# Last layer: the wide projections of the next sequence among the pairs of scores and values, half of the decays ahead of the query with its maxima

## The chip, the cores and the metric

The kernel runs on one core of a Trainium2 chip. The metric is the device time of one execution in microseconds (us). The engines are PE (TensorE, matrix products), DVE (VectorE), ACT (ScalarE), POOL (GpSimd) and SP (SyncE, here only a queue of transfers). Each executes its own instructions in order; semaphores tie them together.

## The reference

A residual stream `x` of 16 sequences, 256 rows each, 128 wide, goes through four layers. Only the last one is touched by the change. For each of its sequences the reference computes, cut to what matters:

```python
xn = layernorm(x)                                   # of the rows of this sequence
# a state space branch ("attn"): gives s
u, z = split(xn @ in_proj_w.T)                      # 256 channels each
xs   = silu(causal_conv4(u) + conv_b)
time_step, B, C = split(xs @ x_proj_w.T)            # 64, 16, 16
delta = softplus(softplus(time_step @ dt_proj_w.T + dt_b) + dt_b)
state_t = exp(delta_t * A) * state_(t-1) + (delta_t * xs_t) * B_t      # 16 states per channel
y  = (sum over states of state_t * C_t + xs * D) * silu(z);  s = y @ out_proj_w.T
# an attention block with experts ("ffn"): gives g
q, k, v = xn @ Wq + bq, ...;  rotary q and k;  16 heads of 8 columns
att = softmax(q k^T / sqrt(8)) v;   x1 = layernorm(xn + att @ Wo + bo) * g1 + be1
moe = top-2 of 8 experts: gelu(x1 @ W1 + b1) @ W2 + b2, weighted by the gates
g  = silu(layernorm(x1 + moe) * g2 + be2)
x  = x + s * g
```

The convolution over four steps is folded into four projections (`u_projT`), so that `u` is a sum of four products of 128 x 256 for each half of the channels, and `z` is one product for each half. The decays are `exp(delta * A)`: 16 states and 2 halves of the channels, which is 32 activations of 128 x 255 per sequence.

## The kernel before, in words

The last layer is `layer3`. A loop goes over the 16 sequences (four per turn of the hardware loop). One turn for sequence n finishes n and prepares n+1. The order of the work is written out by hand, one program per engine. PSUM is one tensor `bank` of eight banks; `back` is banks 0 to 3 and `front` banks 4 to 7. The stages, in order of time:

- **The front stage** (`attention_front` on PE, L2332). Query and key are turned (`turn_heads`, L2284), the scores of 4 blocks of 4 heads are computed (`scores`, L2302), and DVE takes the row maxima of each block (`heads_max`, L2780, 4 instructions). Then DVE finishes `delta` (`softplus_sum`, L2739, in `third_part`), and PE turns the query again, now with its maxima, which ACT copies (`copy_qm`, L2471).
- **The pair stage.** The heads are worked in 8 pairs, p = 0 to 7. PE computes transposed scores of a pair (`scoresT`, L2316, rows of 9), ACT takes the exponential (`exp_scores`, L2518) and behind it one group of four decays for one half of the channels (`decays`, L2510). PE makes the values of a block of two pairs (`heads_out`, L2374). Two sets of two banks alternate for the pairs, so `scoresT` of pair p waits for the exponential of pair p-2. Pairs 0 and 1 belong to the end of the turn before. Also in this stage: PE's `out_rows` (L2325), which gives `s`; ACT's copy of it (L2585), for which DVE waits before it updates `x` (L2923); then DVE's norm of the next sequence, whose last part writes `xn` (L2687), which PE turns after pair 5 (`turn_x`, L2247) and ACT copies after pair 6 (`copy_xnT`, L2468). Meanwhile DVE scans states 0 to 7 (`scan`, L2811) and multiplies by C (`times_c`, L2821).
- **The middle stage.** ACT copies the last values (L2561), PE turns them (L2412), DVE divides (L2845 to L2849), PE projects (L2419, L2423), then come the projections of `u` and `z` for sequence n+1 (`project_uz`, L2257 and L2261), then the first layer norm on DVE, the turning of `x1` (L2430), the router (L2434), and DVE's `route_shift` (L174).
- **The expert stage.** Eight experts, `up` (L2386), `gelu` (L2548) and `down` (L2397), beside the scans of states 8 to 15 and the preparation of n+1 up to `dt`.

PE's two calls around the change are these:

```python
for k in range(2, HP):
    scoresT(n, k)
    if k % 2 == 0:
        heads_out(k // 2 - 1)
    if k == 5:
        turn_x(n + 1, 1 - par)
```

Transfers: SP stores B and C of n+1 to DRAM and loads them broadcast; POOL adds groups of states by accumulating DMAs.

Of the kernel before, what the change touches and what calls it, by code (L numbers as in the profile page):

```python
# [15 lines left out]
P = 128  # L16
NSEQ, T, D = 16, 256, 128
TILES = T // P
# [2063 lines left out]
def layer3(nc, c):  # L2082
    w = c.w3
    with ExitStack() as ctx:
# [156 lines left out]
        def _(pe):  # L2241
# [11 lines left out]

            def project_uz():
                for i in range(CI):
                    for k in range(DCONV):
                        done = nc.tensor.matmul(bank[:, 2, i * T:(i + 1) * T], u_projT[:, i, k, :], xpad[:, k:k + T],  # L2257
                                                start=(k == 0), stop=(k == DCONV - 1))
                done.then_inc(u_in_psum, 1)
                for i in range(CI):  # L2260
                    done = nc.tensor.matmul(bank[:, 3, i * T:(i + 1) * T], z_projT[:, i, :], xnT,  # L2261
                                            start=True, stop=True)
                done.then_inc(z_in_psum, 1)
# [8 lines left out]
            def project_dt(m):  # L2272
                pe.wait_ge(xdbl_ready, m + 1)
                pe.wait_ge(zg_ready, m + 1)
                for i in range(CI):
                    done = nc.tensor.matmul(bank[:, 3, i * T:(i + 1) * T], dt_projT[:, i, :], xdbl[0:RANK, :],
                                            start=True, stop=True)
                done.then_inc(dt_in_psum, 1)
# [77 lines left out]
            for a in range(TILES):  # L2356
                qkv_rows(a)
            project_uz()
            project_x(0, 0)
            project_dt(0)  # L2360
            attention_front(0)
            with pe.Fori(0, NSEQ // 4) as m:
                for q in range(4):
# [50 lines left out]
                    done.then_inc(o_turned, 1)  # L2414
                    pe.wait_ge(xnT_ready, n + 2)
                    qkv_rows(0)
                    pe.wait_ge(y_ready, n + 1)
                    for a in range(TILES):
                        done = nc.tensor.transpose(bank[:, 4, a * P:(a + 1) * P], y[:, a, :], c.ident[:, :])  # L2419
                    done.then_inc(yT_in_psum, 1)  # L2420
                    pe.wait_ge(yT_ready, n + 1)
                    for a in range(TILES):
                        done = nc.tensor.matmul(bank[:, 5, a * D:(a + 1) * D], yT[:, a * P:(a + 1) * P], w.o[:, :],  # L2423
                                                start=True, stop=True)
                    done.then_inc(o_in_psum, 1)
                    project_uz()
                    qkv_rows(1)
                    pe.wait_ge(x1_ready, n + 1)
                    for a in range(TILES):
                        done = nc.tensor.transpose(bank[:, 4, a * P:(a + 1) * P], x1[:, a, :], c.ident[:, :])  # L2430
                    done.then_inc(x1T_in_psum, 1)
                    pe.wait_ge(x1T_ready, n + 1)
                    for a in range(TILES):
                        done = nc.tensor.matmul(bank[:, 5, a * E3:(a + 1) * E3], x1T[:, a * P:(a + 1) * P], w.g[:, :],  # L2434
                                                start=True, stop=True)
# [27 lines left out]
        def _(act):  # L2463
# [16 lines left out]
            def silu_uz(m, par):  # L2480
                act.wait_ge(u_in_psum, m + 1)
                for i in range(CI):
                    done = v.activation(xs[:, par, i, :], bank[:, 2, i * T:(i + 1) * T], ACT.Silu,
                                        bias=w.conv_b[:, i:i + 1])
                done.then_inc(xs_ready, 1)
                act.wait_ge(z_in_psum, m + 1)
                v.activation(zg[:, par, :, :].rearrange("p i t -> p (i t)"), bank[:, 3, :], ACT.Silu)\
                    .then_inc(zg_ready, 1)
# [44 lines left out]
            copy_qk(0)  # L2533
            log_part(0, 1)
            copy_qm(0)
            for p in range(2):
                exp_scores(0, p)
            with act.Fori(0, NSEQ // 4) as m:
                for q in range(4):
# [23 lines left out]
                    act.wait_ge(yT_in_psum, n + 1)  # L2563
                    v.activation(yT[:, :], bank[:, 4, 0:T], ACT.Copy).then_inc(yT_ready, 1)
                    silu_uz(n + 1, 1 - par)
                    act.wait_ge(x1T_in_psum, n + 1)
                    v.activation(x1T[:, :], bank[:, 4, 0:T], ACT.Copy).then_inc(x1T_ready, 1)
                    route_exp(nc, r, n)
# [8 lines left out]
                    copy_qk(n + 1)  # L2577
                    log_part(n + 1, 1)
                    copy_qm(n + 1)
                    act.wait_ge(gate_ready, n + 1)  # L2580
# [80 lines left out]
        def _(dve):  # L2661
# [135 lines left out]
            for blk in range(NBLK):  # L2797
                heads_max(0, blk)
            third_part(0, 0)
            v.drain()  # L2800
# [3 lines left out]
            with dve.Fori(0, NSEQ // 4) as m:  # L2804
                for q in range(4):
# [41 lines left out]
                    for a in range(TILES):  # L2847
# [6 lines left out]
                    dve.wait_ge(resid_ready, n + 1)  # L2854
                    v.tensor_tensor(rows[:, :, :], bank[:, 5, 0:TILES * D].rearrange("p (a d) -> p a d", d=D),
                                    resid[:, :, :], ALU.add).then_inc(rows_ready, 1)
# [5 lines left out]
                    dve.wait_ge(logits_in_psum, n + 1)  # L2862
                    route_shift(nc, r, bank[:, 5, 0:TILES * E3].rearrange("p (a e) -> p a e", e=E3), logits_taken,
                                w.bg[:, :].unsqueeze(1).to_broadcast([P, TILES, E3]))
# [41 lines left out]
                    for blk in range(NBLK):  # L2906
                        heads_max(n + 1, blk)
                    third_part(n + 1, 1 - par)
                    inner_apply(rows[:, :, :], w.g2, w.be2, 2 * n + 2).then_inc(gate_ready, 1)
# [98 lines left out]
```

## Time and profile before

| | us |
|---|---|
| median of 3 runs | 2950.62 (2947.14 to 2953.3) |
| the profiled execution | 2951.83 |
| span of the core in it | 2950.1 |
| busy: PE / DVE / ACT / POOL | 2500.4 / 2327.4 / 1689.7 / 336.4 |
| granted clock of PE, mean of the span | 0.854 of full speed |

Lines (L...) are lines of the kernel before. A granted clock of 1.00 is 2.4 GHz, 0.50 is 1.2 GHz. PE's busy time is modelled at its ends, so starts of consecutive instructions are the safer measure. "idle before" in a timeline is the engine's idle time before an instruction, and behind the arrow stands what ended it. Timeline rows merge like instructions; the second number is the time from the first start to the last end. One turn of a sequence in the last layer takes some 86 us; the turn shown below is one of sixteen.

### The profile page before, as it was taken

What the parts mean: (1) busy time and instruction counts of PE and PEld (TensorE: products, weight loads), DVE (VectorE), ACT (ScalarE), POOL (GpSimd) and SP (SyncE); (2) the same over time, 40 slices, a digit from 0 to 9 for tenths busy, and PEclk for the clock granted to TensorE, in tenths of its full rate; (3) what the DMA queues carried; (4) which work ended last, traced back from release to release, by engine and by line L of the source; (5) the groups of instructions that cost most, each with busy time, mean ns of one, the idle gap of its engine ahead of it and who ended that gap; (6) DMA issues with size and microseconds to landing.
All of it is one profiled execution on the core that took longest, in us unless ns stands there. A gap on an engine that the chain in (4) does not pass through costs nothing. (4 is left out here: it accounts for less than half of the span.)

```text
span 2950.1 us, 55763 instructions
## 1 busy us (share of the span) xinstructions
PE 2500.4 (85%) x18940; PEld 1896.2 (64%) x18940; DVE 2327.4 (79%) x6064; ACT 1689.7 (57%) x3432; POOL 336.4 (11%) x357
## 2 busy tenths in 40 slices
PE   1899998899999999776649888888988888888886
PEld 1666666677777777655636666666665666666665
DVE  1899998788788888675257888888888888888887
ACT  1677776556565566443326565655656565565654
POOL 0000000000000000033121111111111111111111
PEclk9999999899999999888858777788776778877777
DMA  7000000000000000210214323343433334443334
GB/s 220 2 0 0 0 0 0 1 2 0 1 0 1 0 1 0 64 27 27 58 55 106 93 73 86 88 108 94 108 87 75 88 89 107 95 102 84 76 91 110
DMA packets 86524, 163.77 MB, mean 56 GB/s; under 512 B 18856, under 2 KB 45617, under 8 KB 86321
## 3 DMA queue, kind: packets, MB, share of 16 engines
q0 software_dynamic: 20480, 62.93, 11.2%
q1 hardware_dynamic: 64640, 98.15, 10.3%
q8 instruction: 94, 1.54, 0.2%
q14 instruction: 110, 0.89, 0.1%
q10 hardware_dynamic: 1200, 0.27, 0.1%
HBM read 92.60 MB, written 9.99 MB: 35 GB/s over the span
## 5 line engine op out<-in xcount | busy, mean ns | idle before, releaser
L1140 ACT ACTIVATE b_neg<-b_neg,b_nmax 128x128 f32<-128x128 f32 (+1 forms) x512 | 190.9, 444 | 205.6 <-DVE b_nmax L1294 205.6
L2548 ACT ACTIVATE d_probs<-l_bank,w_b 128x256 f32<-128x256 f32 x512 | 210.8, 469 | 155.6 <-PE l_bank L2386 153.3
L2811 DVE TENSOR_TENSOR_SCAN d_state<-w,d_state 128x1024 f32<-128x1024 f32 x128 | 290.9, 2284 | 3.8 <-issue 3.4
L2386 PE MATMUL l_bank<-xnT,w_w 128*128 128x256 f32 x1024 | 245.1, 382 | 13.8 <-ACT d_probs L2548 13.8
L2397 PE MATMUL l_bank<-w_w,d_probs 128*128 128x128 f32 x2048 | 252.6, 276 | 0.0
L2397 PEld LDWEIGHTS l_bank<-w_w,d_probs 128*128 128x128 f32 x2048 | 244.9, 192 | 11.7 <-ACT d_probs L2548 5.3
L2316 PE MATMUL l_bank<-w 9*128 9x256 f32 x1040 | 208.8, 669 | 25.5 <-ACT w L2471 18.9
L2510 ACT ACTIVATE w<-d_delta,w_A_log 128x255 f32<-128x255 f32 x520 | 220.2, 498 | 0.0
L94 POOL TENSOR_TENSOR ln_rstd<-ln_var_eps,minus_half 128x2 f32<-128x2 f32 x51 | 70.6, 1384 | 1293.1 <-DVE ln_var_eps L88 1293.1
L2386 PEld LDWEIGHTS l_bank<-xnT,w_w 128*128 128x128 f32 x1024 | 184.7, 190 | 40.5 <-ACT d_probs L2548 20.7
L2316 PEld LDWEIGHTS l_bank<-w 9*128 9x128 f32 x1040 | 123.7, 320 | 96.0 <-issue 32.3
L1294 DVE CUSTOM_DVE_ANT_0 b_neg<-l_bank,causal 128x128 f32<-128x128 f32 (+1 forms) x512 | 151.9, 353 | 32.3 <-PE l_bank L989 16.4
L2780 DVE TENSOR_REDUCE d_qk<-l_bank 128x8 f32<-128x2048 f32 x68 | 152.7, 2288 | 5.5 <-PE l_bank L2302 4.5
L2821 DVE TENSOR_TENSOR d_state<-d_state,d_bct 128x1024 f32<-128x1024 f32 x128 | 151.1, 1222 | 6.3 <-issue 2.7
L1015 PEld LDWEIGHTS l_bank<-down,b_fused 128*128 128x128 f32 x1024 | 123.9, 191 | 50.1 <-issue 29.8
L2302 PE MATMUL l_bank<-w 8*128 8x256 f32 x1088 | 113.1, 562 | 48.5 <-ACT w L2477 25.0
L1015 PE MATMUL l_bank<-down,b_fused 128*128 128x128 f32 x1024 | 148.2, 288 | 6.9 <-DVE b_y L1326 6.3
L2787 DVE TENSOR_TENSOR d_state<-d_bct,d_du 128x1024 f32<-128x1024 f32 x132 | 153.9, 1218 | 0.1
L2616 POOL DMA_DIRECT2D d_state<-d_state x96 | 85.6, 1046 | 588.9 <-DVEq L2823 476.5
L2374 PE MATMUL l_bank<-d_probs,d_vaug 128*32 128x256 f32 x1024 | 123.9, 634 | 30.9 <-ACT d_probs L2518 30.9
L2471 ACT ACTIVATE w<-l_bank 128x1024 f32<-128x1024 f32 x34 | 34.8, 1024 | 198.8 <-PE l_bank L2284 198.8
L2518 ACT ACTIVATE d_probs<-l_bank 128x1024 f32<-128x1024 f32 x130 | 132.1, 1016 | 24.1 <-PE l_bank L2316 24.1
(404 smaller groups left out, 5699.2 us busy)
## 6 DMA issues: line engine op xcount, KB each, us to landing
d_bct<-l_bc SPq DMA_DIRECT2D x132, 512.0 KB, 4.0
d_state<-d_state POOLq DMA_DIRECT2D x96, 512.0 KB, 6.7
d_state<-d_state POOLq DMA_DIRECT2D x32, 256.0 KB, 4.0
x_sorted<-x SPq DMA_DIRECT2D x1, 2560.0 KB, 16.7
w<-in_L_ffn_w_dram SPq DMA_DIRECT2D x1, 2048.0 KB, 10.3
w_w<-in_L_ffn_W_dram SPq DMA_DIRECT2D x1, 2048.0 KB
c2e_xg<-x_sorted SPq DMA_DIRECT2D x16, 128.0 KB
y_sorted<-c2e_yo SPq DMA_DIRECT2D x16, 128.0 KB, 1.8
```

What stands on the lines that cost most here:

```text
L1015: done = nc.tensor.matmul(bank[:, 7, a * D:(a + 1) * D], fused[:, e % 2, f * T + a * P:f * T + (a + 1) * P], c.down1[:, e, f, :], start=(f ...
L1140: done = nc.scalar.activation(neg[:, slot, cols], neg[:, slot, cols], ACT.Exp, bias=nmax[:, slot, a:a + 1], scale=-1.0)
L1294: done = v.tensor_tensor_reduce(neg[:, slot, lo:hi], bank[:, 1 + b, lo:hi], c.causal[:, lo:hi], -SCALE, 3e38, ALU.add, ALU.min, nmax[:, sl ...
L2316: done = nc.tensor.matmul(back[:, 2 * (p % 2) + i, j * T:(j + 1) * T], kT[own, blk, j * P:(j + 1) * P], qT[own, blk, :], start=True, stop= ...
L2386: done = nc.tensor.matmul(bank[:, b, i * T:(i + 1) * T], w.w1[:, e, k * P:(k + 1) * P], x1T[:, :], start=True, stop=True)
L2397: done = nc.tensor.matmul(bank[:, 4 + e % 2, a * D:(a + 1) * D], hid[:, e % 2, k, a * P:(a + 1) * P], w.w2[:, e, k, :], start=(k == 0), st ...
L2510: done = v.activation(dA[i][:, g % (NG - 1), k, 1:T], delta[:, i, 1:T], ACT.Exp, scale=negA[:, i, SG * g + k:SG * g + k + 1])
L2548: done = v.activation(hid[:, e % 2, k, :], bank[:, b, i * T:(i + 1) * T], ACT.Gelu, bias=w.b1[:, e, k:k + 1])
L2780: v.tensor_reduce(qk[:, :, 0, GR * blk:GR * (blk + 1), HD3].rearrange("p a h -> p h a"), banks.rearrange("p h (a t) -> p h a t", a=TILES), ...
L2787: done = v.tensor_tensor(st[i][:, SG * g:SG * (g + 1), :], bct[:, g, :, :], du[:, i, :].unsqueeze(1).to_broadcast([P, SG, T]), ALU.mult)
L2811: done = v.tensor_tensor_scan(group, dA[i][:, g % (NG - 1), :, :].rearrange("p m t -> p (m t)"), group, 0.0, ALU.mult, ALU.add)
L2821: done = v.tensor_tensor(group, group, bct[:, g, :, :], ALU.mult)
```

## The change

1. **PE, projections moved.** `project_uz` is split in `project_u(0)`, `project_u(1)` and `project_z`. They leave the middle stage and go among the pairs: `project_u(0)` behind pair 5, `project_u(1)` behind pair 6 and its block of values, `project_z` behind pair 7 and ahead of the last block of values. The wait for the turned rows (`xnT_ready`) moves with them.
2. **PE, `turn_x` moved** from behind pair 5 to behind pair 3; ACT copies its result behind the exponential of pair 4, not 6.
3. **ACT, decays moved.** Groups 0 and 1 (16 of 32 activations) go behind `log_part(.., 1)` and ahead of `copy_qm`, that is, into the front stage. Groups 2 and 3 stay in the pair stage, behind the odd pairs only.
4. **DVE.** The second `softplus_sum` moves from behind the four maxima to behind the first.
5. **Banks.** `u` goes to bank 4 and `z` to bank 5; the turned `y` and `x1` and what follows from them go to banks 2 and 3. Waits change accordingly: `down(0)` waits for `xs_ready`, `down(1)` for `zg_ready`, `project_dt` for `logits_taken`.

The activations of `u` and `z` (`silu_uz`) stay at their place in ACT's program.

```diff
+            def project_u(i):
+                for k in range(DCONV):
+                    done = nc.tensor.matmul(bank[:, 4, i * T:(i + 1) * T], u_projT[:, i, k, :], xpad[:, k:k + T],
+                                            start=(k == 0), stop=(k == DCONV - 1))
+                if i == CI - 1:
+                    done.then_inc(u_in_psum, 1)
+
+            def project_z():
...
-                    done = nc.tensor.matmul(bank[:, 3, i * T:(i + 1) * T], z_projT[:, i, :], xnT,
+                    done = nc.tensor.matmul(bank[:, 5, i * T:(i + 1) * T], z_projT[:, i, :], xnT,
...
             def project_dt(m):
                 pe.wait_ge(xdbl_ready, m + 1)
-                pe.wait_ge(zg_ready, m + 1)
+                if later(m):
+                    pe.wait_ge(logits_taken, m)
...
+                        if e == 0:
+                            pe.wait_ge(xs_ready, n + 2)
                         if e == 1:
-                            pe.wait_ge(logits_taken, n + 1)
+                            pe.wait_ge(zg_ready, n + 2)
...
                         if k % 2 == 0:
                             heads_out(k // 2 - 1)
+                        if k == 3:
+                            turn_x(n + 1, 1 - par)
                         if k == 5:
-                            turn_x(n + 1, 1 - par)
+                            pe.wait_ge(xnT_ready, n + 2)
+                            project_u(0)
+                        if k == 6:
+                            project_u(1)
+                        if k == 7:
+                            project_z()
...
-                    pe.wait_ge(xnT_ready, n + 2)
                     qkv_rows(0)
...
-                    project_uz()
                     qkv_rows(1)
...
# ACT
                              scale=float(HD3) ** -0.5).then_inc(probs_ready, 1)
-                decays(n, p // 2, p % 2)
+                if p % 2:
+                    decays(n, 2 + p // 4, p // 2 % 2)
...
-                        if p == 6:
+                        if p == 4:
                             copy_xnT(n + 1)
...
                     log_part(n + 1, 1)
+                    for k in range(4):
+                        decays(n + 1, k // 2, k % 2)
                     copy_qm(n + 1)
...
# DVE
             def third_part(m, par):
-                softplus_sum(m, 1)
                 v.tensor_tensor(du[:, :, :], delta[:, :, :], xs[:, par, :, :], ALU.mult)
...
                     for blk in range(NBLK):
                         heads_max(n + 1, blk)
+                        if blk == 0:
+                            softplus_sum(n + 1, 1)
```

## Rows read from the trace of the kernel before

**Rows 1.** Windows: busy time of each engine by stage of one sequence, granted clock (PEclk).

```profile
core 0: us, PE busy (x) PEld busy (x) DVE busy (x) ACT busy (x) POOL busy (x), PEclk, DMA share, GB/s
...
2412.00:2437.50 25.50, 22.82 (x138) 12.13 (x138) 22.96 (x27) 23.71 (x47) 2.65 (x1) 0.50 0.14 42
2437.60:2443.30 5.70, 5.23 (x18) 3.84 (x19) 3.42 (x7) 1.67 (x2) 1.80 (x2) 0.50 0.73 138
2443.40:2481.50 38.10, 37.07 (x233) 32.76 (x233) 31.85 (x83) 20.86 (x44) 5.25 (x7) 1.00 0.56 146
```

**Rows 2.** Waits of DVE, 1633 to 2930 us: waiter, releaser, total us, times, longest.

```profile
DVE until L2845 <- PE l_bank L2412: 29.4, 15, 2.3
DVE d_y L2923 <- ACT xnT L2585: 15.2, 15, 1.3
```

**Rows 3.** Timeline of DVE, 2399 to 2428 us: start, us, engine, line, operation, idle before.

```profile
2399.95 9.00 DVE L2780 TENSOR_REDUCE d_qk<-l_bank 128x8 f32<-128x2048 f32 x4 [0.53 <-PE l_bank L2302]
2408.86 0.68 DVE L2739 SCALAR_TENSOR_TENSOR d_delta<-d_dv,d_dneg 128x512 f32<-128x512 f32 x1
...
2419.70 0.42 DVE L2923 SCALAR_TENSOR_TENSOR d_y<-d_x,same_head 128x256 f32<-128x256 f32 x1 [0.92 <-ACT xnT L2585]
...
2424.85 0.61 DVE L2687 TENSOR_SCALAR d_xn<-x,ln_meanvar,ln_rstd 128x128 f32 x2 [0.52 <-POOL ln_rstd L94]
```

**Rows 4.** Timeline of ACT, 2397 to 2450 us.

```profile
2411.00 1.02 ACT L2471 ACTIVATE w<-l_bank 128x1024 f32<-128x1024 f32 x1 [10.22 <-PE l_bank L2284]
...
2414.20 1.02 ACT L2518 ACTIVATE d_probs<-l_bank 128x1024 f32<-128x1024 f32 x1 [0.45 <-PE l_bank L2316]
2415.12 1.69 ACT L2510 ACTIVATE w<-d_delta,w_A_log 128x255 f32<-128x255 f32 x4
...
2419.21 0.37 ACT L2585 ACTIVATE xnT<-l_bank 128x256 f32<-128x256 f32 x1
...
2436.94 0.60 ACT L2561 ACTIVATE l_attn<-l_bank 128x512 f32<-128x512 f32 x1 [0.47 <-PE l_bank L2374]
```

**Rows 5.** Timeline of PE, 2411 to 2450 us.

```profile
2412.08 2.11 PE L2316 MATMUL l_bank<-w 9*128 9x256 f32 x16 [1.11 <-ACT w L2471]
...
2416.30 2.08 PE L2316 MATMUL l_bank<-w 9*128 9x256 f32 x8
2418.30 1.94 PE L2374 MATMUL l_bank<-d_probs,d_vaug 128*32 128x256 f32 x16
2420.17 2.45 PE L2316 MATMUL l_bank<-w 9*128 9x256 f32 x16
2423.37 1.94 PE L2374 MATMUL l_bank<-d_probs,d_vaug 128*32 128x256 f32 x16 [0.75 <-ACT d_probs L2518]
...
2427.25 0.69 PE L2247 MATMUL l_bank<-ident,d_xn 128*128 128x128 f32 x2
...
2437.59 1.97 PE L2412 MATMUL l_bank<-ident,l_attn 128*128 128x128 f32 x8 [0.72 <-ACT l_attn L2561]
2439.35 1.49 PE L2251 MATMUL l_bank<-w_qkv,d_xpad 128*128 128x384 f32 x2
...
2442.76 3.92 PE L2257 MATMUL l_bank<-d_xpad,d_u_projT 128*128 128x256 f32 x16
...
2448.02 0.38 PE L2430 MATMUL l_bank<-ident,d_x 128*128 128x128 f32 x2
```

**Rows 6.** Timeline of DVE, 2430 to 2451 us.

```profile
2439.60 0.37 DVE L2845 RECIPROCAL until<-l_bank 128x16 f32<-128x16 f32 x2 [2.29 <-PE l_bank L2412]
...
2443.01 0.42 DVE L2855 TENSOR_TENSOR same_head<-l_bank,xn 128x256 f32<-128x256 f32 x1 [0.21 <-PE l_bank L2423]
...
2449.60 0.17 DVE L174 TENSOR_TENSOR same_head<-l_bank,w_bg 128x16 f32<-128x16 f32 x1
```

**Rows 7.** Windows at the same place of the last sequence.

```profile
2870.10:2873.30 3.20, 3.20 (x11) 2.31 (x12) 1.17 (x5) 0.00 (x0) 1.80 (x2) 0.50 0.53 101
2873.50:2876.00 2.50, 2.03 (x13) 1.72 (x12) 2.41 (x5) 1.67 (x2) 0.00 (x0) 1.00 1.09 205
```

More of the change, by code:

```diff
@@ L2252, in qkv_rows @@
                     .then_inc(qkv_in_psum, 1)
-            def project_uz():
-                for i in range(CI):
[L2256 to L2260, printed above, removed]
-                    done = nc.tensor.matmul(bank[:, 3, i * T:(i + 1) * T], z_projT[:, i, :], xnT,
+            def project_u(i):
[5 more added lines that the diff above has]
+            def project_z():
+                for i in range(CI):
+                    done = nc.tensor.matmul(bank[:, 5, i * T:(i + 1) * T], z_projT[:, i, :], xnT,
                                             start=True, stop=True)
@@ L2357, in _ @@
                 qkv_rows(a)
-            project_uz()
+            for i in range(CI):
+                project_u(i)
+            project_z()
             project_x(0, 0)
@@ L2405, in _ @@
                             heads_out(k // 2 - 1)
+                        if k == 3:
+                            turn_x(n + 1, 1 - par)
                         if k == 5:
-                            turn_x(n + 1, 1 - par)
+                            pe.wait_ge(xnT_ready, n + 2)
[3 more added lines that the diff above has]
+                        if k == 7:
+                            project_z()
                     heads_out(NBLK - 1)
@@ L2418, in _ @@
                     for a in range(TILES):
-                        done = nc.tensor.transpose(bank[:, 4, a * P:(a + 1) * P], y[:, a, :], c.ident[:, :])
+                        done = nc.tensor.transpose(bank[:, 2, a * P:(a + 1) * P], y[:, a, :], c.ident[:, :])
                     done.then_inc(yT_in_psum, 1)
@@ L2422, in _ @@
                     for a in range(TILES):
-                        done = nc.tensor.matmul(bank[:, 5, a * D:(a + 1) * D], yT[:, a * P:(a + 1) * P], w.o[:, :],
+                        done = nc.tensor.matmul(bank[:, 3, a * D:(a + 1) * D], yT[:, a * P:(a + 1) * P], w.o[:, :],
                                                 start=True, stop=True)
                     done.then_inc(o_in_psum, 1)
-                    project_uz()
                     qkv_rows(1)
@@ L2429, in _ @@
                     for a in range(TILES):
-                        done = nc.tensor.transpose(bank[:, 4, a * P:(a + 1) * P], x1[:, a, :], c.ident[:, :])
+                        done = nc.tensor.transpose(bank[:, 2, a * P:(a + 1) * P], x1[:, a, :], c.ident[:, :])
                     done.then_inc(x1T_in_psum, 1)
@@ L2433, in _ @@
                     for a in range(TILES):
-                        done = nc.tensor.matmul(bank[:, 5, a * E3:(a + 1) * E3], x1T[:, a * P:(a + 1) * P], w.g[:, :],
+                        done = nc.tensor.matmul(bank[:, 3, a * E3:(a + 1) * E3], x1T[:, a * P:(a + 1) * P], w.g[:, :],
                                                 start=True, stop=True)
@@ L2482, in silu_uz @@
                 for i in range(CI):
-                    done = v.activation(xs[:, par, i, :], bank[:, 2, i * T:(i + 1) * T], ACT.Silu,
+                    done = v.activation(xs[:, par, i, :], bank[:, 4, i * T:(i + 1) * T], ACT.Silu,
                                         bias=w.conv_b[:, i:i + 1])
@@ L2486, in silu_uz @@
                 act.wait_ge(z_in_psum, m + 1)
-                v.activation(zg[:, par, :, :].rearrange("p i t -> p (i t)"), bank[:, 3, :], ACT.Silu)\
+                v.activation(zg[:, par, :, :].rearrange("p i t -> p (i t)"), bank[:, 5, :], ACT.Silu)\
                     .then_inc(zg_ready, 1)
@@ L2534, in _ @@
             log_part(0, 1)
+            for k in range(4):
+                decays(0, k // 2, k % 2)
             copy_qm(0)
@@ L2563, in _ @@
                     act.wait_ge(yT_in_psum, n + 1)
-                    v.activation(yT[:, :], bank[:, 4, 0:T], ACT.Copy).then_inc(yT_ready, 1)
+                    v.activation(yT[:, :], bank[:, 2, 0:T], ACT.Copy).then_inc(yT_ready, 1)
                     silu_uz(n + 1, 1 - par)
                     act.wait_ge(x1T_in_psum, n + 1)
-                    v.activation(x1T[:, :], bank[:, 4, 0:T], ACT.Copy).then_inc(x1T_ready, 1)
+                    v.activation(x1T[:, :], bank[:, 2, 0:T], ACT.Copy).then_inc(x1T_ready, 1)
                     route_exp(nc, r, n)
@@ L2578, in _ @@
                     log_part(n + 1, 1)
+                    for k in range(4):
+                        decays(n + 1, k // 2, k % 2)
                     copy_qm(n + 1)
@@ L2798, in _ @@
                 heads_max(0, blk)
+                if blk == 0:
+                    softplus_sum(0, 1)
             third_part(0, 0)
@@ L2854, in _ @@
                     dve.wait_ge(resid_ready, n + 1)
-                    v.tensor_tensor(rows[:, :, :], bank[:, 5, 0:TILES * D].rearrange("p (a d) -> p a d", d=D),
+                    v.tensor_tensor(rows[:, :, :], bank[:, 3, 0:TILES * D].rearrange("p (a d) -> p a d", d=D),
                                     resid[:, :, :], ALU.add).then_inc(rows_ready, 1)
@@ L2862, in _ @@
                     dve.wait_ge(logits_in_psum, n + 1)
-                    route_shift(nc, r, bank[:, 5, 0:TILES * E3].rearrange("p (a e) -> p a e", e=E3), logits_taken,
+                    route_shift(nc, r, bank[:, 3, 0:TILES * E3].rearrange("p (a e) -> p a e", e=E3), logits_taken,
                                 w.bg[:, :].unsqueeze(1).to_broadcast([P, TILES, E3]))
@@ L2907, in _ @@
                         heads_max(n + 1, blk)
+                        if blk == 0:
+                            softplus_sum(n + 1, 1)
                     third_part(n + 1, 1 - par)
```

## Prediction

> **What bounds the kernel now.** I read the windows by stage first [rows 1]. In the turn shown the pair stage (2412 to 2437.5) has PE 22.8 of 25.5 us busy and ACT 23.7, at a granted clock of 0.50, that is 1.2 GHz; the middle stage begins at 0.50 and passes to 1.00 (2.4 GHz) at about 2443.35; the expert stage has PE 37.1 of 38.1 busy at 1.00. DVE has waits at few places, so I read them next [rows 2]: 29.4 us in 15 turns for the turned values (L2412), 2.3 in the longest, and 15.2 us in 15 turns for ACT's copy of `s` (L2585). Outside the experts these two are DVE's main waits, and between them DVE works almost without a pause. So a turn gets shorter where the copy of `s` or the turned values come earlier, and longer by every microsecond by which the turned values come later.
>
> The pair stage then has to be read as a chain through PE and ACT. ACT [rows 4]: an exponential takes 0.92 us from start to start (2414.20 to 2415.12), a group of decays behind it 1.69, of which 1.6 count. PE [rows 5], at 1.2 GHz: a pair alone takes 2.0 (2416.30 to 2418.30), a block of values 1.87 (2418.30 to 2420.17), pairs 3 and 4, issued together, 2.45 in all. The waits that PE's rows show here are 0.75 and its like, each for ACT. The two engines are about equally long, and that is where the change acts.
>
> **The parts of the change.**
>
> *Decays moved ahead.* 4 groups x 1.6 = 6.4 us of ACT leave the pair stage. In the front stage ACT is idle for 10.22 us ahead of `copy_qm` [rows 4], beside DVE's four maxima [rows 3]. Delta is now ready after the first maximum: 2399.95 + 9.0/4 + 0.77 = 2403.0, so the groups end at 2409.5. `copy_qm` could start at 2411.0, so the cost is nothing, with 1.5 us of cover; without that cover each microsecond would delay pairs 0 and 1.
>
> *softplus_sum moved.* DVE does the same work. But the last maximum, and with it `copy_qm`, comes 0.77 later (its 0.68, and 0.1 as an estimate for the drain) [rows 3]: `copy_qm` at 2411.8, pairs 0 and 1 at 2412.85 instead of 2412.08.
>
> *The copy of s.* Exponential 0 at 2414.97, exponential 1 at 2415.9, one group of decays instead of two, the copy at 2418.4 instead of 2419.21 [rows 4]. DVE reaches L2923 at 2418.8, so 0.85 of its 0.92 wait goes [rows 3]. The next rows `xn` are ready at 2418.85 + 5.7 = 2424.6 (5.7 from 2419.70 to the end of L2687, the wait for POOL in it unchanged). What DVE gains it loses again if it has to wait for the turned values.
>
> *turn_x two pairs earlier.* PE [rows 5]: pairs 0 and 1 at 2412.85; `out_rows`, pair 2 at 2416.8, block 0 at 2418.8, pair 3 at 2420.6, done 2422.6. There it now waits for `xn` until 2424.6: 2.0 us of idle PE, and behind it, in order, pair 4, all further pairs and blocks. Pair 4 also loses its company: together with pair 3 it cost 0.45 more, alone it costs 2.0. Turning (0.6) puts pair 4 at 2425.2, block 1 at 2427.2, pair 5 at 2429.1, done at 2431.1. ACT has meanwhile done exponentials 2 to 4 and the copy of the turned rows (2428.8), so it holds nothing up.
>
> *The projections.* The trace of before has the 16 instructions of `u` largely at 2.4 GHz: 3.92 for 16, less the tail of the last, is 0.235 each [rows 5]. At 1.2 GHz the nearest row is the turning of the values, 8 products of 128 columns between the starts 2437.59 and 2439.35, so 0.22 each and 0.43 for 256 columns. Half of `u` is 8 instructions: 1.9 us as the lower bound, 3.4 as the upper one; I take 3.4 for `project_u(0)`, since all of the pair stage has 0.50 [rows 1], and for the rest it depends on when the clock rises. In the turn shown the 128-row products start at 2437.59 and the clock is 0.50 until 2443.3, with 5.2 us of such products [rows 1, 5]; in the last sequence the same products start at 2870.1 and at 2873.5 it is 1.00, after 3.2 us of them [rows 7]. So it rises with the end of `project_u(0)` in the earlier of the two, and 1.8 us into `project_u(1)` in the other.
>   - Early rise, 2434.5: pair 6 to 2435.6, block 2 to 2436.6, `project_u(1)` 1.9 to 2438.5, pair 7 to 2439.65 (half of the durations at 1.2 GHz with a tenth on top, as 0.235 to 0.427 shows), exponential 7 to 2440.6, decays to 2442.2. `project_z` and block 3 hide beside these. Copy 0.6, turned values 1.0: DVE can go on at 2443.8 instead of 2439.60 [rows 6], 4.2 later.
>   - Late rise: pair 6 to 2436.5, block 2 to 2438.4, `project_u(1)` to 2441.1 (1.8 at the low clock, the other 4 instructions at 0.235), pair 7 to 2442.2, exponential 7 to 2443.2, decays to 2444.8, copy and turning to 2446.4: 6.8 later.
>
> The clock's rule in the Trainium skill, "TensorE: Matmul & The Clock Gate", Part 1, is that throttling is the default and activity releases it, and that the monitor looks at how busy PE has been. The pair stage speaks against reading that as the profile's busy share: PE is 89% busy at 0.50 there [rows 1]. What that rule would give if busy time alone counted is the third rival.
>
> *The middle stage.* `project_uz` leaves a stretch in which DVE is the one that works: from 2439.60 to 2449.60 the only wait for PE is 0.21, for the projected values [rows 6]. `x1` is turned at 2448.02 [rows 5] and could now be 0.5 earlier, but L174, which uses what follows, starts without a wait [rows 6]. Five us of PE work leave and buy 0.21, because behind them stands DVE, not PE. The gelus start from L174 as before, so the experts gain nothing. The new waits of `down(0)`, `down(1)` and `project_dt` are met by then; bounds 0 and, if the activations of `u` and `z` came as late as the router, about 1 us; I take 0, as ACT is idle there.
>
> **Sum.** Early 4.2 - 0.2 = 4.0, late 6.8 - 0.2 = 6.6 per turn; with 6 to 4 for the early one 5.0. Sixteen turns: +80 us. The profiled execution has 2951.8 (span 2950.1 and 1.7 around it), which would become 3032; it lies 1.2 above the median, so the forecast is 3031. Its own range is 16 x 4.0 to 16 x 6.6: 3015 to 3056.
>
> **Rivals.**
> - *The clock rises as soon as the projections begin* (slower, less): from 2431.1 on at 2.4 GHz, `project_u(0)` to 2433.0, pair 6 to 2434.1, block 2 to 2435.1, `project_u(1)` to 2437.0, pair 7, exponential and decays to 2440.7, turned values at 2442.4: +2.8 - 0.2 = 2.6, x 16 = +42, 2993. For it: blocks of values just ahead may count. Against: the two rises shown.
> - *It does not rise before the turned values* (slower, more): both halves of `u` 3.4, pair 7 to 2443.8, `project_z`, block 3 to 2447.4, turned values 2450: +10.4, x 16 = +166, 3117. Against: 5.2 us of 128-row work sufficed where it is shown, and the two halves have 6.8.
> - *The high clock covers the whole pair stage* (faster). The mechanism: denser work in the pairs holds 2.4 GHz from the front stage on. Then ACT sets the pace, pair 4 goes at 2424.9, exponential 7 ends at 2435.5, decays 2437.1, turned values at 2438.8: 0.8 earlier, with the 0.2 that is 1.0 per turn, -16, 2935. It decides at pair 3: if PE is at 1.00 there, the change wins. Against: the front stage is unchanged in kind, and the work ahead of `project_u(0)` is what was there at 0.50.
> - *No change.* PE overlaps pairs with blocks once ACT does not hold them (as pairs 3 and 4 did), which would give back some 4 to 5 us per turn: 2950. Against: pair 2 and block 0 lay 2.0 apart although both were ready [rows 5].
>
> **How the numbers follow.** Forecast 0.64, rise at once 0.13, no rise 0.06, high clock throughout 0.10, no change 0.07. A difference of 0.2% is about what a measurement of this kernel tells from none: 2944.7 to 2956.5. Faster 0.11 (the third rival and a little of the fourth), same 0.05, slower 0.84. The range for 8 times in 10 takes in the forecast and the first rival with a margin of some 20 us for the prices taken at the wrong clock: 2972 to 3072.
>
> **What would show it.** PE: an idle time of about 2 us ahead of `turn_x`, released by DVE's `xn`; `project_u(0)` at 0.43 per instruction, `project_u(1)` mostly at 0.235; the clock rising between 2.5 and 9 us after the start of `project_u(0)`. DVE: no wait left for the copy of `s`, and the wait ahead of L2845 of 2.3 grown to 7 to 10 us. ACT: idle between the exponentials, no longer ahead of `copy_qm` for more than 2.5 us. Experts and front stage as long as before. The forecast is wrong if the wait for the turned values stays under 3 us, if `turn_x` finds `xn` ready, or if pairs and projections run side by side.

## The result and the profile after

| | before | after |
|---|---|---|
| median, us | 2949.72 (4 runs) | 3049.3 (3046.84 to 3050.51, 4 runs) |
| ratio to before | | 1.0336, 95% interval 1.0318 to 1.0354 |
| span of the profiled execution, us | 2950.1 | 3048.8 |
| mean granted clock | 0.854 | 0.858 |

The change makes the kernel 3.4% slower, by 99.6 us, which is 6.2 in each of 16 turns. It was forecast as 3031 with a range of 2972 to 3072. A run over 1.5% above the fastest of its own kernel does not count into a ratio, though it does into a median: none here, but in the experiments below the profiled execution of 6, one of 8 and four of 12, its profiled one among them. The mean clock is a little higher than before, so its mean over the span says nothing about this loss; where it is high and low does.

DVE's waits after, over 15 turns, 1633 to 3030 us (waiter, releaser, total us, times, longest); they answer to [rows 2]. The waits of the experiments below are from the same stretch. The third row is from the kernel before, for the second:

```profile
DVE until L2863 <- PE l_bank L2426: 117.1, 15, 10.6
DVE same_head L2847 <- PE l_bank L2404: 74.4, 45, 2.2
DVE same_head L2829 <- PE l_bank L2397: 52.4, 45, 2.0
```

The wait for the turned values grew from 29.4 to 117.1 us, 5.85 per turn. The wait for the copy of `s`, 15.2 before, is gone from the list: 1.0 per turn gained. The second row is the wait for the `down` of the first expert and of the last two. It was 52.4 us in 45 waits before and is 74.4, and the growth is at the first expert: 1.47 per turn, which the prediction doesn't have. The 0.21 ahead of the projected values is gone too, and a wait of 0.17 is new between the first two maxima. Sum: 5.85 + 1.47 - 1.01 - 0.21 + 0.17 = 6.27, times 16 is 100, against 99.6 measured.

One turn after, by windows (the columns of [rows 1], PEclk third from the end). The first is the pair stage, the next two are parts of it, then the middle stage, the stretch from the turned `x1` to the end of the first `up`, and the other experts:

```profile
core 0: us, PE busy (x) PEld busy (x) DVE busy (x) ACT busy (x) POOL busy (x), PEclk, DMA share, GB/s
2478.50:2505.50 27.00, 24.09 (x143) 13.99 (x143) 18.22 (x20) 14.03 (x27) 4.44 (x3) 0.68 0.33 78
2492.80:2495.80 3.00, 3.00 (x9) 2.45 (x8) 2.92 (x3) 2.87 (x6) 0.00 (x0) 0.50 0.03 5
2496.00:2504.50 8.50, 7.51 (x62) 4.31 (x60) 2.12 (x2) 4.12 (x8) 1.79 (x2) 1.00 0.53 101
2505.70:2513.00 7.30, 2.41 (x10) 0.95 (x8) 6.52 (x18) 3.00 (x5) 1.40 (x2) 1.00 0.23 73
2513.10:2519.70 6.60, 5.96 (x16) 4.51 (x17) 6.13 (x16) 4.61 (x8) 0.00 (x0) 0.50 0.25 79
2519.90:2548.80 28.90, 28.90 (x197) 26.34 (x196) 22.49 (x56) 14.85 (x34) 4.38 (x6) 1.00 0.60 148
```

PE in this turn (start, us, line, idle before); L2319 are the pairs, L2256 `project_u`, L2247 `turn_x`, L2426 the turned values, L2442 the turned `x1`, L2391 `up`. It answers to [rows 5]:

```profile
2482.39 2.08 PE L2319 MATMUL l_bank<-w 9*128 9x256 f32 x8
2486.32 0.69 PE L2247 MATMUL l_bank<-ident,d_xn 128*128 128x128 f32 x2 [1.85 <-DVE d_xn L2704]
2486.93 2.08 PE L2319 MATMUL l_bank<-w 9*128 9x256 f32 x8
...
2492.82 3.51 PE L2256 MATMUL l_bank<-d_xpad,d_u_projT 128*128 128x256 f32 x8
2496.26 1.13 PE L2319 MATMUL l_bank<-w 9*128 9x256 f32 x8
...
2498.32 2.00 PE L2256 MATMUL l_bank<-d_xpad,d_u_projT 128*128 128x256 f32 x8
2500.25 1.13 PE L2319 MATMUL l_bank<-w 9*128 9x256 f32 x8
...
2504.57 1.09 PE L2426 MATMUL l_bank<-ident,l_attn 128*128 128x128 f32 x8 [1.00 <-ACT l_attn L2576]
...
2508.15 0.81 PE L2251 MATMUL l_bank<-w_qkv,d_xpad 128*128 128x384 f32 x2
2513.26 0.69 PE L2442 MATMUL l_bank<-ident,d_x 128*128 128x128 f32 x2 [4.30 <-DVE d_x L2791]
...
2515.30 3.76 PE L2391 MATMUL l_bank<-xnT,w_w 128*128 128x256 f32 x8
...
2520.20 1.89 PE L2391 MATMUL l_bank<-xnT,w_w 128*128 128x256 f32 x8
```

Pair 3 starts at 2482.39, and `turn_x` only at 2486.32, after 1.85 us of idle time, released by `xn` on DVE. `project_u(0)` takes 3.4 us for 8 instructions, at 0.50. The clock is 1.00 from 2496 on, with the end of it; pair 6 then has 1.06, `project_u(1)` 1.9. Further down is the unforeseen part: PE ends `qkv_rows(1)` at 2508.96 and idles 4.30 us until `x1`. The window from 2513.1 has 0.50, and in it `up(0)` takes 3.76, against 1.89 for `up(1)` at 2520.20, at 1.00. Before, the same stretch was busy with `project_uz` (L2257 in [rows 5]) and at 1.00 [rows 1]. DVE in the same turn; the rows answer to [rows 6], and the last is the first expert's sum:

```profile
2505.70 0.37 DVE L2863 RECIPROCAL until<-l_bank 128x16 f32<-128x16 f32 x2 [7.58 <-PE l_bank L2426]
...
2508.82 0.42 DVE L2873 TENSOR_TENSOR same_head<-l_bank,xn 128x256 f32<-128x256 f32 x1
...
2523.91 0.61 DVE L2847 SCALAR_TENSOR_TENSOR same_head<-l_bank,until,d_x 128x128 f32<-128x128 f32 x2 [2.14 <-PE l_bank L2404]
```

The turned values end a wait of 7.58 instead of 2.29; the projected values are there at once; the first expert's sum waits 2.14. Before, it waited 0.67:

```profile
2456.56 0.61 DVE L2829 SCALAR_TENSOR_TENSOR same_head<-l_bank,until,d_x 128x128 f32<-128x128 f32 x2 [0.67 <-PE l_bank L2397]
```

ACT (answers to [rows 4]): the last exponential and the decays behind it, then the 16 decays in the front stage with the idle time ahead of `copy_qm`:

```profile
2501.43 1.02 ACT L2530 ACTIVATE d_probs<-l_bank 128x1024 f32<-128x1024 f32 x1 [2.96 <-PE l_bank L2319]
2502.35 1.69 ACT L2522 ACTIVATE w<-d_delta,w_A_log 128x255 f32<-128x255 f32 x4
...
2556.46 6.47 ACT L2522 ACTIVATE w<-d_delta,w_A_log 128x255 f32<-128x255 f32 x16 [1.69 <-DVE d_delta L2756]
2565.45 1.02 ACT L2483 ACTIVATE w<-l_bank 128x1024 f32<-128x1024 f32 x1 [2.52 <-PE l_bank L2287]
```

### The profile page after: what moved, and what is told of

It is laid out like the page before. It is cut to its first block and busy times, and to the rows that moved or that the text cites. A ratio compares the mean times of both kernels' runs of the same rounds, so it can differ in the third digit from the quotient of the medians.

```text
span 3048.8 us, 55774 instructions
## 1 busy us (share of the span) xinstructions
PE 2518.4 (83%) x18940; PEld 1908.3 (63%) x18940; DVE 2328.4 (76%) x6064; ACT 1702.5 (56%) x3444; POOL 338.0 (11%) x357
## 5 line engine op out<-in xcount | busy, mean ns | idle before, releaser
L2391 PE MATMUL l_bank<-xnT,w_w 128*128 128x256 f32 x1024 | 272.1, 413 | 0.0
L2319 PE MATMUL l_bank<-w 9*128 9x256 f32 x1040 | 206.0, 605 | 24.1 <-ACT w L2483 18.9
L2391 PEld LDWEIGHTS l_bank<-xnT,w_w 128*128 128x128 f32 x1024 | 204.0, 209 | 27.3
L2319 PEld LDWEIGHTS l_bank<-w 9*128 9x128 f32 x1040 | 119.8, 287 | 93.3 <-issue 28.3
L2633 POOL DMA_DIRECT2D d_state<-d_state x96 | 85.4, 1043 | 612.2 <-DVEq L2841 499.7
L997 PE MATMUL l_bank<-b_xnT,gating 128*128 128x256 f32 x512 | 135.0, 387 | 3.3 <-DVE b_gated L1311 3.3
L1003 PE MATMUL l_bank<-b_xnT,up 128*128 128x256 f32 x512 | 133.2, 383 | 0.0
```

What stands on the lines that cost most here:

```text
L2319: done = nc.tensor.matmul(back[:, 2 * (p % 2) + i, j * T:(j + 1) * T], kT[own, blk, j * P:(j + 1) * P], qT[own, blk, :], start=True, stop= ...
L2391: done = nc.tensor.matmul(bank[:, b, i * T:(i + 1) * T], w.w1[:, e, k * P:(k + 1) * P], x1T[:, :], start=True, stop=True)
```

## Experiments

Each experiment was set up with two theories, A and B, and what each would give. At first they were these. A: PE is the bound of the pair stage, and what counts is its stall, its order and its clock. B: instructions count as such, wherever they are. The unread products in some kernels below are `matmul(bank[:, b, 0:256], w1[:, 0, 0:128], w1[:, 1, 0:256])`, written `fill(b, count)`; they cost 0.47 us each at 2.4 GHz and 0.86 at 1.2. All ratios are to the kernel before on the same chip.

**1. turn_x behind pair 4.**

```diff
-                        if k == 3:
+                        if k == 4:
                             turn_x(n + 1, 1 - par)
```

> Change as measured, but turn_x behind pair 4 and its block of values instead of behind pair 3. Theory A (PE is the bound of the pair stage, by its wait for xn and by the projections at the low clock): the idle 1.85 us ahead of turn_x goes, and pairs 3 and 4 go together again (some 1.6 us), so the turned values come 3.4 us earlier in each of 16 turns: some 54 us less than the changed kernel, 2995. Theory B (the wait ahead of turn_x is hidden, only the projections cost): no more than 10 us less than the changed kernel, 3040 or more.

Measured: 3030.1 us, ratio 1.0266 (1.0248 to 1.0283). That is 19 us less than the change, between both theories, and neither number came out. PE in one turn, and the windows behind it:

```profile
2479.93 3.78 PE L2256 MATMUL l_bank<-d_xpad,d_u_projT 128*128 128x256 f32 x8
2483.64 2.08 PE L2319 MATMUL l_bank<-w 9*128 9x256 f32 x8
2485.65 1.94 PE L2379 MATMUL l_bank<-d_probs,d_vaug 128*32 128x256 f32 x16
2487.52 2.83 PE L2256 MATMUL l_bank<-d_xpad,d_u_projT 128*128 128x256 f32 x8
...
2494.60 1.09 PE L2426 MATMUL l_bank<-ident,l_attn 128*128 128x128 f32 x8 [1.00 <-ACT l_attn L2576]
```

```profile
2483.60:2489.00 5.40, 5.40 (x29) 3.00 (x29) 4.29 (x3) 1.03 (x1) 0.41 (x1) 0.50 0.00 0
2489.30:2494.00 4.70, 4.24 (x33) 2.34 (x31) 0.00 (x0) 2.55 (x6) 1.08 (x2) 1.00 0.89 169
```

The stall is gone and `project_u(0)` starts 2.7 us earlier in the turn (9.6 behind DVE's update of `x`, 12.3 in the changed kernel). But here the clock does not rise with its end: pair 6, block 2 and the beginning of `project_u(1)` are at 0.50 too. The clock rises 9.3 us after the start of `project_u(0)`, in the changed kernel 3.1. Of the last 15 waits for the turned values in this trace five are 4.0 to 4.2 and ten are 7.4 to 7.8. The five have the rise 2.8 to 3.9 us after that start, the ten 9.2 to 9.5. So the 3.4 us that theory A expected are there where the clock rises early and are taken back where it rises late: the moment of the rise is worth as much as the stall.

**2. The middle stage filled.**

```diff
                     qkv_rows(1)
+                    for _ in range(8):
+                        nc.tensor.matmul(bank[:, 2, 0:T], w.w1[:, 0, 0:P], w.w1[:, 1, 0:T], start=True, stop=True)
                     pe.wait_ge(x1_ready, n + 1)
```

> Change as measured, plus 8 products of 128 x 256 whose result nobody reads, on PE in the middle stage where it otherwise idles 4.3 us for x1. Theory A (the late start of the experts comes from PE's clock, which falls to 1.2 GHz because the projections no longer fill this idle time): the clock stays at 1.00 until the experts, DVE's wait ahead of its first expert goes from 2.1 back to about 0.7, so 16 x 1.47 = 24 us less than the changed kernel, 3026. Theory B (the late start is the order of the work: the new waits of down(0) and down(1), or the other banks): no change, 3049, or more where the fill delays x1.

Measured: 3047.3, ratio 1.0329 (1.0311 to 1.0346). By the time alone theory A would have failed. The trace says otherwise, first DVE's waits, then the middle stage and the beginning of the experts by its window:

```profile
DVE until L2865 <- PE l_bank L2426: 136.6, 15, 10.3
DVE same_head L2849 <- PE l_bank L2404: 52.4, 45, 2.0
```

```profile
2508.00:2520.00 12.00, 9.62 (x52) 7.75 (x51) 10.48 (x35) 7.09 (x14) 1.40 (x2) 1.00 0.27 90
```

The experts' waits are back at 52.4, exactly as before, and the clock stays at 1.00: this part of A is shown. But the turned values now wait 136.6 instead of 117.1. In the changed kernel three of four turns lasted 92.1 us and the fourth, where the hardware loop branches, 95.9; 14 of the 15 had the early rise, the first the late one, with a wait of 10.6. Here turns of 91 and 93 us (the fourth 97) follow each other, with waits of 8.1 and 10.3: the clock rises 4.0 to 4.5 us after the start of `project_u(0)` in the first kind and 8.7 to 9.0 in the second. So 22 us are won at the experts and 19.5 lost at the pairs.

**3. The decays alone.** The kernel before with the change's ACT and DVE part.

```diff
-                decays(n, p // 2, p % 2)
+                if p % 2:
+                    decays(n, 2 + p // 4, p // 2 % 2)
```

> Kernel before with the ACT and DVE part of the change alone: half of the decays ahead of the query with its maxima, softplus_sum behind the first maximum; PE as before. Theory A (PE, not ACT, then sets the pair stage at 1.2 GHz): the copy of s comes earlier, DVE's wait for it of 1.0 goes, and the wait for the turned values grows by as much; within 0.3% of the kernel before, 2945 to 2955. Theory B (ACT was the bound of the pair stage): 6.4 us of ACT leave it and DVE's waits of 2.0 and 1.0 go, some 40 us less than before, 2910.

Measured: 2957.0, ratio 1.0022 (1.0012 to 1.0032). DVE's waits:

```profile
DVE same_head L2835 <- PE l_bank L2397: 52.4, 45, 2.0
DVE until L2851 <- PE l_bank L2412: 47.4, 15, 3.7
```

The wait for the copy of `s` is gone (15.2) and the one for the turned values grew by 18.0. The last maximum comes 0.85 us later than before, and the pairs start as much later. From the start of pair 0 to the turned values taken by DVE, a common turn has 27.35 us, against 27.52 before. So 6.4 us less of ACT in the pair stage bought 0.17: PE was the bound. This is theory A, at 2 us above its range, with the later maxima as a small loss.

**4. The projections alone.** The changed kernel with all decays among the pairs, as before.

```diff
-                if p % 2:
-                    decays(n, 2 + p // 4, p // 2 % 2)
+                decays(n, p // 2, p % 2)
```

> Changed kernel without its ACT and DVE part: all decays stay among the pairs, softplus_sum behind the last maximum; the projections, turn_x and banks as changed. Theory A (PE is the bound there and ACT's decays lie in its waits, but for the two ahead of the copy of s, which delay xn and with it turn_x by 1.6 - 0.8 us): 10 to 20 us more than the changed kernel, 3060 to 3070. Theory B (both parts count alike): 6.4 us of ACT come back into the stage, 16 x 6.4 = 100 us more, 3150.

Measured: 3092.3, ratio 1.0487 (1.0469 to 1.0504), 43 more than the change. Both expectations missed:

```profile
DVE until L2857 <- PE l_bank L2426: 146.8, 15, 10.4
DVE same_head L2841 <- PE l_bank L2404: 69.6, 43, 2.0
DVE d_y L2935 <- ACT xnT L2597: 15.3, 15, 1.3
```

The second row has 43 of 45 waits, since two lie behind 3030 us. The wait for the copy of `s` is back (1.0 per turn), and DVE waits 9.8 us per turn for the turned values instead of 7.8, although `project_u(0)` starts at the same distance behind the copy of `s`. In 12 of 15 turns of this trace the clock rises 9 us after that start, not 3. The parts are not additive: decays +6.5, projections +142, both +100 us. But the decays' part hardly helps by itself here either. Where the rise is early in both kernels, in the fourth turns, these last 95.8 to 95.9 us in both. Where it is late in both they last 95.4 to 95.6 here and 95.1 in the one such turn of the changed kernel. What makes the 43 us is that late rises are 12 of 15 here and 1 of 15 there, and no run shows why.

**5 to 7. The clock held up through the pairs.** All three have `fill` behind the third maximum (2), behind the turned query (1), ahead of pair 2 (2) and behind pairs (2 each). The edit below is the part in the pair stage, as 6 and 7 have it.

```diff
+                    fill(4, 2)
                     for k in range(2, HP):
                         scoresT(n, k)
+                        fill(4, 2)
```

5 is on the changed kernel (behind pairs 2 to 4 only, and 8 in the middle stage), 6 on the kernel of experiment 3, 7 on the kernel before.

> Change as measured, plus products of 128 x 256 whose result nobody reads, wherever PE waits or works with few rows: two behind the third maximum, one behind the turned query, two ahead of pair 2, two each behind pairs 2, 3 and 4, eight in the middle stage. Theory A (the change loses because PE goes through the pair stage at 1.2 GHz; the third rival of the prediction is its reverse): the clock is at 1.00 from pair 2 or 3 on, DVE's wait for the turned values falls from 7.6 to 2 to 3 us, the wait ahead of the experts to 0.7: 2935 to 2955. Theory B (the pair stage is too long by its instructions at either clock): the added products come on top, 3060 or more.

> Decays and softplus_sum as in the change, projections, turn_x and banks as in the kernel before, plus the same kind of unread products: two behind the third maximum, one behind the turned query, two ahead of pair 2 and two behind each of pairs 2 to 7. Theory A (at 2.4 GHz neither PE nor ACT bounds the pair stage once half of the decays are out of it, and DVE does): the turned values are there when DVE asks, its wait of 3.2 goes, 16 x 3.0 less than the decays alone, 2905 to 2920. Theory B (the clock does not rise early enough, or falls again between the pairs): PE has 12 to 20 us more per turn at 1.2 GHz, 3000 or more.

> Kernel before with the unread products of the run before this one and nothing of the change. Theory A: the clock is up in the pair stage, but ACT with all 32 decays sets its length; the turned values come some 1 us earlier, 2925 to 2950. Theory B (ACT never bounds it, the clock alone does): as fast as with the decays moved, 2905 to 2920.

Measured: 5 is 3014.9, ratio 1.0225 (1.0208 to 1.0242); 6 is 2942.7, ratio 0.9972 (0.9948 to 0.9997), with single runs from 2918.5 to 2988.2; 7 is 2990.5, ratio 1.0143 (1.0126 to 1.0160). DVE's waits in 5:

```profile
DVE until L2874 <- PE l_bank L2436: 99.1, 15, 9.7
DVE same_head L2858 <- PE l_bank L2411: 55.1, 45, 2.0
```

They are 1.2 per turn less for the turned values than in the changed kernel, and at the experts nearly as before: 34 of the 100 us are won back, where theory A wanted all and B none. In 6 the turns differ, so two windows of its pair stages and the two waits for the turned values (L2860) that belong to them are the best reading; the profiled execution is the longest of ten, 2988.2, so its share of long turns does not stand for the others:

```profile
2346.00:2362.00 16.00, 14.94 (x119) 9.00 (x116) 14.87 (x16) 10.89 (x20) 2.65 (x1) 1.00 0.09 32
2432.00:2456.00 24.00, 24.00 (x101) 13.45 (x94) 12.52 (x10) 9.26 (x16) 2.79 (x3) 0.50 0.23 44
```

```profile
2360.20 2.36 DVE L2836 TENSOR_TENSOR d_state<-d_state,d_bct 128x1024 f32<-128x1024 f32 x2
2362.70 0.37 DVE L2860 RECIPROCAL until<-l_bank 128x16 f32<-128x16 f32 x2
...
2460.40 0.37 DVE L2860 RECIPROCAL until<-l_bank 128x16 f32<-128x16 f32 x2 [14.90 <-PE l_bank L2421]
```

In the turn at 1.00 the turned values are there when DVE comes (no idle time before 2362.70), and the turn lasts 83.0 us, 3 less than before, as theory A has it. In the turn at 0.50 the same products cost twice as much and nothing hides them: a wait of 14.9 and a turn of 98.1.

Of the 14 turn lengths in this trace eight are 82.8 to 83.9, one is 90.2 and five are 98 to 101. Over the ten executions the time goes roughly with the mean granted clock, from 2918.5 at 0.926 to 2988.2 at 0.900, so the fast ones are likely to have more of the short turns; no trace of one is kept.

In 7 two turns last 83.4 and 83.7, seven some 85.4, and the worst 101. The two short ones have the clock at 1.00 for a larger part of their pair stage and wait 0.2 and 0.6 us for the turned values, with all decays in the pairs. So this trace does not show that ACT holds the good turns back, and that the decays must be moved for a turn of 83 us is not shown. Neither theory's number came out, in 6 or in 7.

**8 to 12. One block to raise the clock.** 8 is the kernel of experiment 3 with five products in one stretch behind `out_rows` and none in the front stage:

```diff
+                    fill(4, 5)
                     for k in range(2, HP):
                         scoresT(n, k)
+                        if k < 7:
+                            fill(4, 2)
```

9 is 8 with the three of the front stage added. 10 is the changed kernel with `turn_x` behind pair 4, the block, two behind each of pairs 2 to 4, and eight products in the middle. 11 is 8 with two behind pairs 2 to 4 only, 12 is 8 with one behind each of pairs 2 to 6.

> Decays and softplus_sum as in the change, projections and turn_x as before, and the unread products placed otherwise: none in the front stage, five in one stretch between out_rows and pair 2 (with out_rows 6 us of 128-row work at 1.2 GHz, more than the 5.2 that sufficed in the trace of before), two behind each of pairs 2 to 6. Theory A (the clock decides, and the run before it was uneven because in some turns it did not rise): all turns are the short ones of 83 to 84 us, against 86.2 before; 2905 to 2920. Theory B (the long turns have another cause, as the fall in the front stage): long turns of 98 us stay, 2940 or more.

> The run before it with the three unread products of the front stage added again. Theory A: they add nothing, since the clock rises behind out_rows anyway; within 10 us of it. Theory B (they are what makes the clock rise in time): faster by more than 10 us.

> Changed kernel with turn_x behind pair 4, the five products between out_rows and pair 2, two behind each of pairs 2 to 4, eight in the middle stage. Theory A (the changed kernel loses by the clock alone): with PE at 2.4 GHz from pair 2 on, the projections cost 1.9 each and the turned values come before DVE asks or little later; 2905 to 2940, faster than before. Theory B (the projections make the stage too long even so): 2960 or more.

> As the run with five unread products between out_rows and pair 2, but two more only behind each of pairs 2, 3 and 4, none behind 5 and 6. Theory A (there the added products themselves, 1.9 us of PE, held back the turned values by 2.4 us): the turned values come 1.9 earlier in every turn, 2915 to 2945, faster than the kernel before. Theory B (the clock falls again without them): the wait for the turned values stays or grows, 2960 or more.

> As that run, but one unread product instead of two behind each of pairs 2 to 6. Theory A: 2.3 us of PE less per turn and the clock still up, 2910 to 2940. Theory B (half as many don't hold the clock): it falls in the midst of the pairs in most turns, 2960 or more.

Measured: 8 is 2971.3 (2951.3 to 3011.1), ratio 1.0058 (1.0040 to 1.0076); 9 is 2974.7, 1.0088 (1.0073 to 1.0104); 10 is 2995.6, 1.0146 (1.0131 to 1.0162); 11 is 2972.7, 1.0065 (1.0037 to 1.0093); 12 is 2972.3, 1.0032 (1.0000 to 1.0065). DVE's waits in 8, and the one for the turned values in 10 and in 12:

```profile
DVE same_head L2842 <- PE l_bank L2401: 52.7, 45, 2.0
DVE until L2858 <- PE l_bank L2419: 45.8, 15, 5.9
```

```profile
DVE until L2871 <- PE l_bank L2433: 94.3, 15, 14.1
DVE until L2858 <- PE l_bank L2419: 70.3, 15, 12.5
```

With the block no turn of 98 us is left in the trace of 8 (84.8 to 89.6; its profiled execution is the shortest, 2951.3, and of the longest, 3011.1, there is no trace), and in 8 of its 15 turns the clock is at 1.00 from within 2 us of DVE's update of `x` to the turned values. So the block does raise the clock. But its products and the ten behind it are 7 us at 2.4 GHz, and DVE waits 3.1 us per turn for the turned values, more than the 2.0 before. With fewer behind it (11, 12) the clock falls among the pairs: turns of 84.0 beside 91.3 and 99.1 in 12.

Experiment 10 answers whether the changed kernel loses by the clock alone. In nine of its 15 turns the clock is at 1.00 over that same stretch. They last 87.4 to 88.7 us, against 84.8 to 85.5 for the eight of 8. The rise is a little later in most of them; where it comes at the same place, 0.4 to 0.7 us ahead of the update, they last 87.4 and 87.6 against 85.4 to 85.5. Yet 10 has four unread products fewer in its pair stage. So with the projections in it this stage is some 2 us longer at 2.4 GHz too.

Expectation A of 8, 10, 11 and 12 failed. B held for the last three; for 8 its time held, but its turns of 98 us are not in the trace. In 9 the front products made 3 us of difference, as A has it. No version here is faster than before by more than the 0.3% of experiment 6, whose interval nearly reaches 1.

## Why the prediction was right

- **PE's stall ahead of `turn_x`.** Forecast 2.0, measured 1.85. The following steps came out within some tenths of a microsecond, counted from the first step of DVE's update of `x` (2418.85 in the forecast, 2480.5, L2943, in the turn shown): `project_u(0)` at 12.3, forecast 12.3; turned values taken at 25.2, forecast 24.95 for the early rise.
- **The clock.** Forecast as an early and a late rise, 6 to 4. In the changed kernel it was the early one in 14 of 15 turns. The late one, 27.6 by forecast, is what experiment 2 shows in every second turn (27.8). The two distances from the update of `x` to the turned values were therefore right and the shares wrong. The Trainium skill, "TensorE: Matmul & The Clock Gate", Part 1, says that activity releases the throttle. In this trace PE is 24.1 of 27.0 us busy in the pair stage, and its clock is at 0.50 for the first 17 of them, so a busy PE alone did not raise it.
- **The decays and the copy of `s`.** Forecast as free and worth 0.85 per turn, which the pair stage takes back; experiment 3 shows this (1.0 gained, 1.2 lost), and the idle time ahead of `copy_qm` is 2.52.
- **The middle stage: the step that was wrong.** "The gelus start from L174 as before, so the experts gain nothing" held for the order of the work but not for the clock. Without `project_uz` PE idles 4.3 us, the clock falls, and the first `up` takes 3.76 us: 1.47 per turn, 24 us in all, where the prediction had "Experts and front stage as long as before". The account per turn: 4.0 forecast for the early rise, 1.47 here, 0.17 between the maxima, 0.8 more for the turned values (0.25 to 0.55 in the common turns, more in each fourth, where the wait before was shorter, and in the first, where the rise was late), less 0.16 for the copy of `s`, makes 6.3. The forecast's mean was 5.0 and 6.2 was measured. It had counted 4 late rises in 10 and one in 15 came, which hid a part of the miss: that the time came out within 18 us of the forecast is in part luck. Experiment 2 shows the cause: with the gap filled, the waits are 52.4 again.
- **The rivals.** "The high clock covers the whole pair stage" named what would have made it faster, but its price was too kind: experiments 5 and 10 hold the clock up for much of the stage and stay 1.5 to 2.3% above the kernel before, with the cost of the fills in it, and the turns of 10 at the high clock are 1.4 to 2.7 longer than the 86.0 before. "It does not rise before the turned values" leaves out the 0.2 that the other sums take off (10.2 per turn, 3114); nothing rests on it. Overlap of pairs and blocks did not show: pair 4 and block 1 lie 2.0 apart after too.

What stays open is why the clock rises 3 us after the start of `project_u(0)` in some turns and 9 in others. PE's work ahead of it does not settle it: the changed kernel and experiment 4 have it in the same order, and `project_u(0)` starts 12.3 us behind the update of `x` in both, with 14 early rises of 15 in the one and 3 of 15 in the other. The length of the turn does not settle it either: in experiment 1, 12 of 14 turns last 92.0 to 92.3 us, and each fourth of them has the early rise, the others the late. So the times of most experiments tell in part where the rise happened to fall, and small differences between their ratios say little about the edits. A kernel with the rise forced to one place by other means than more products was not tried.

## What to carry to other kernels

Ask of each piece of PE work that is moved what clock it leaves and what clock it enters. Here `project_uz` cost 0.2 us per turn where it stood, hid behind DVE, and kept the experts' start at 2.4 GHz; among pairs of few rows it ran at 1.2 GHz on the path that sets the end. And before an engine is relieved, see whether its partner in the stage is equally long: 6.4 us taken from ACT were worth 0.17 while PE had as much to do.

## What the runs showed of the hardware

- PE's clock can turn a change of a few microseconds into one several times as large or into nothing: experiment 1 took 2.7 us out ahead of the projections, and 10 of 15 turns gave it back, for the clock rose 9.2 to 9.5 us after the start of `project_u(0)` and not 3.1.
- Turns settled into a fixed pattern with the clock: 92.1 us for three of four turns in the changed kernel, 92.0 to 92.3 for 12 of 14 turns in experiment 1, 91.0 and 93.1 in experiment 2. In experiment 6 they spread over 83 to 101. A mean over turns hides this; the list of single turns shows it.
- A gap of 4.3 us in PE's work, in a stretch where PE was busy for 2.4 of 7.3 us, was followed by a clock of 0.50 and cost the next stage 1.47 us per turn; with eight unread products in the gap the clock stayed at 1.00 and the cost was gone (experiment 2).
- With unread products the same program spread over 2918 to 2988 us in ten executions (experiment 6), where the kernel before stayed within 2947 to 2952 beside it.
